# First convolution of a two-layer MoE network: the shared convolution in the turned image's PSUM banks, token logits from the finished image, top two of four by a 4x4 table

## What is computed

```python
# first convolution, on x normalised over channels per pixel
pooled = mean(x, (2, 3));  h = silu(pooled @ router_w1.T + router_b1)
probs = softmax(h @ router_w2.T + router_b2)            # 4 experts
top_v, top_i = top_k(probs, 2);  w = top_v / sum(top_v);  w = where(w >= 0.01, w, 0)
shared = silu(group_norm(einsum('oc,bchw->bohw', shared_w, x)))
expert_e = silu(group_norm(conv3x3(x, expert_w[e])))    # two of four are computed
x = x0 + shared + w0 * expert_{i0} + w1 * expert_{i1}
# first feed-forward network, on tokens (pixels) normalised over channels
probs = softmax(layernorm(t) @ router_w.T)              # 8 experts, two per token
gates = top2 / (sum(top2) + 1e-9)
y = sum over the two: gate * (silu(t w1) * (t w3)) w2
```

## Time and profile before

| | us |
|---|---|
| median of 3 runs | 2041.85 |
| lowest and highest | 2039.49, 2042.02 |
| the profiled execution | 2049.27 |
| its span on the core | 2047.5 |
| PE, DVE, ACT, POOL busy | 1725.7, 1474.9, 1029.6, 1055.8 |

### The profile page before, as it was taken

The page is one execution under the profiler, slowest core; times in us unless marked ns, Lnnn a source line. Parts: engine busy times, 40 slices in busy tenths (PEclk is TensorE's granted clock), DMA queues, the critical chain, the costliest instruction groups (busy, mean ns, idle before and its releaser), DMA issues.

```text
span 2047.5 us, 40915 instructions
## 1 busy us (share of the span) xinstructions
PE 1725.7 (84%) x9314; PEld 962.7 (47%) x9315; DVE 1474.9 (72%) x5423; ACT 1029.6 (50%) x1740; POOL 1055.8 (52%) x1198
## 2 busy tenths in 40 slices
PE   2679889988988849999999995589898959999957
PEld 2334444444444424555555552355555534444447
DVE  5777677776767656777777774777777657888857
ACT  1444344434434426777777773245656525555524
POOL 1003445435544646777777776435666444666620
PEclk8689999998999969999999998689989979999979
DMA  8600111111111124222222221312221013222146
GB/s 265 174 11 31 45 36 42 40 42 40 44 34 35 38 64 114 80 82 75 82 81 77 82 67 49 103 34 82 72 63 44 26 48 111 78 80 79 35 116 213
DMA packets 180063, 149.06 MB, mean 73 GB/s; under 512 B 19302, under 2 KB 161822, under 8 KB 179960
## 3 DMA queue, kind: packets, MB, share of 16 engines
q1 hardware_dynamic: 153336, 98.05, 17.5%
q0 software_dynamic: 26624, 49.93, 7.2%
HBM read 76.00 MB, written 77.34 MB: 75 GB/s over the span
## 4 chain that ended last, share of the span: by engine, by line
PE 54%; DVE 16%; issue 11%; ACT 9%; DMA 4%; POOL 3%; ACTq 1%; SPq 1%; DVEq 0%; POOLq 0%
PE banks L759 12%; PE banks L760 12%; PE banks L761 12%; PE banks L754 9%; PE banks L975 5%; ACT work L1091 4%; POOL slot_rows L626 2%; ACT work L1190 2%; PE banks L772 1%; DMA slot_rows<-work,small 1%; PE banks L985 1%; DVE small L1471 1%; DMA wb_h<-ffn_rows 1%; DVE small L1496 1%; DVE small L1467 1%
## 5 line engine op out<-in xcount | busy, mean ns | idle before, releaser
L647 POOL DMA_INDIRECT ffn_rows<-work x448 | 486.1, 1085 | 238.8 <-issue 170.0
L626 POOL DMA_INDIRECT slot_rows<-work,small x384 | 389.6, 1015 | 327.3 <-DVE small L1668 146.8
L754 PE MATMUL banks<-small,work 128*128 128x128 f32 x1344 | 197.3, 285 | 179.3 <-ACT work L1091 153.2
L754 PEld LDWEIGHTS banks<-small,work 128*128 128x128 f32 x1344 | 159.7, 146 | 251.4 <-issue 142.3
L1891 DVE TENSOR_TENSOR work<-work 128x512 f16<-128x512 f32 x376 | 260.8, 694 | 12.6
L759 PE MATMUL banks<-work,wb_h 128*128 128x512 f16 x648 | 247.4, 382 | 6.1 <-issue 4.5
L761 PE MATMUL banks<-work,wb_l 128*128 128x512 f16 x648 | 247.3, 382 | 0.0
L760 PE MATMUL banks<-work,wb_h 128*128 128x512 f16 x648 | 247.2, 382 | 0.0
L759 PE MATMUL banks<-work,wa_h 128*128 128x512 f16 x576 | 235.1, 408 | 3.6 <-ACT work L1122 3.2
L1907 DVE SCALAR_TENSOR_TENSOR work<-banks,small,work 128x512 f32<-128x512 f32 x216 | 161.4, 747 | 102.9 <-ACT work L1204 102.3
L760 PE MATMUL banks<-work,wa_h 128*128 128x512 f16 x576 | 234.5, 407 | 0.0
(11 more groups left out here) (323 smaller groups left out, 3203.2 us busy)
## 6 DMA issues: line engine op xcount, KB each, us to landing
wa_l<-slot_rows SPq DMA_DIRECT2D x112, 264.0 KB, 2.9
work<-ffn_rows SPq DMA_DIRECT2D x32, 512.0 KB, 5.3
work<-in_x SPq DMA_DIRECT2D x16, 512.0 KB, 3.4
ffn_rows<-small SPq DMA_DIRECT2D x32, 256.0 KB, 3.8
out_image<-work SPq DMA_DIRECT2D x16, 512.0 KB, 3.1
ffn_rows<-work POOLq DMA_INDIRECT x448, 2.2
slot_rows<-work,small POOLq DMA_INDIRECT x384, 2.3
slot_rows<-small SPq DMA_DIRECT2D x17, 264.0 KB, 4.2
```

The costliest lines, as they stand in the source:

```text
L626: pool_e.indirect_dma_start(slots, bass.IndirectOffsetOnAxis(ap=slot_i[:, row_buffer(p, i, k), tt:tt + 1], axis=0), rows[row_buffer(p, i, ...
L647: pool_e.indirect_dma_start(dst, bass.IndirectOffsetOnAxis(ap=idg[old.v][:, qq, 0:1].bitcast(I32), axis=0), yt[old.u][:, qq, :], None, bou ...
L754: last = pe.transpose(dst[:, tt * P:(tt + 1) * P], x, ident)
```

## The change

- The shared convolution (j = 0) now lands in `tp` (banks 0 and 1), by a new function `home(j)`; its statistics and SiLU read there. The next image's transposes now wait for that SiLU (`A_silu0`); the first expert convolution of the step waits for `A_silu1` of the image before in place of `A_silu0`.
- On PE a step now begins with the loads of the two expert numbers and two taps, then the transposes of the loaded image. The shared convolution of `nxt` stands ahead of the small product of its gates. `group_mean(old, 2)` stands behind four taps instead of three.
- Token logits: the router's weights are centred over channels once in the setup (three VectorE instructions, one transpose, one copy). The logits then come straight from the finished image `acc` right behind its transposes, and are multiplied by the token's 1/deviation on VectorE. `route_turn` and the ScalarE copy behind it (lines 1107) go, for stage A.
- Token choice: both picks are done in one chain on the logits themselves; the exponentials of all eight and of the second pick are one instruction behind it. The rest of the routing moved: the second pick from step i+1 to step i, the placing behind the image's statistics, woven with the last accumulation.
- Image gates: rank by a 4x4 table of differences; expert numbers, affine constants and exponentials picked in one product and one sum.
- On ScalarE the normalised tokens and their exponentials stand behind both SiLU instructions of the step instead of between.

```diff
+        def home(j):
+            return tp if j == 0 else pair[of(j)]
...
             def conv_half(i, j, half, regs, taps=range(TAPS)):
-                dst = pair[of(j)][:, half * 512:(half + 1) * 512]
+                dst = home(j)[:, half * 512:(half + 1) * 512]
...
+            def a_logits(i):
+                if some(i.b):
+                    pe.wait_ge(sem("A_pos_read"), i.b)
+                for tt in range(TPI):
+                    last = pe.matmul(sm_b[:, tt * E:(tt + 1) * E], acc[i.u][:, tt * P:(tt + 1) * P], rw_centred, start=True, stop=True)
+                last.then_inc(sem("A_logits_done"), 1)
...
             def a_step(i):
...
-                    turn(tp, [xcm[nxt.u][:, tt * P:(tt + 1) * P] for tt in range(TPI)]).then_inc(sem("A_xt_done"), 1)
                 if live(i, IMAGES):
                     pe.wait_ge(sem("A_gate_ready"), i.b + 1)
                     regs += [pe.value_load(eidx[0:1, i.u, k:k + 1], min_val=0, max_val=EC - 1) for k in range(2)]
-                    pe.wait_ge(sem("A_silu0"), i.b + 1)
-                    conv_half(i, 1, 0, regs, range(3))
+                    if some(i.b):
+                        pe.wait_ge(sem("A_silu1"), i.b)
+                    conv_half(i, 1, 0, regs, range(2))
+                if live(nxt, IMAGES):
+                    if some(nxt.b):
+                        pe.wait_ge(sem("A_silu0"), nxt.b)
+                    turn(tp, [xcm[nxt.u][:, tt * P:(tt + 1) * P] for tt in range(TPI)]).then_inc(sem("A_xt_done"), 1)
+                if live(i, IMAGES):
+                    conv_half(i, 1, 0, regs, range(2, 4))
                 if live(old, IMAGES):
                     group_mean(old, 2)
...
                     turn(tp, [acc[old.u][:, tt * P:(tt + 1) * P] for tt in range(TPI)]).then_inc(sem("A_tok_done"), 1)
+                    a_logits(old)
...
-                    conv_half(i, 2, 0, regs, range(5, 8))
+                    conv_half(i, 2, 0, regs, range(5, 7))
                 if live(nxt, IMAGES):
+                    pe.wait_ge(sem("A_padl_done"), nxt.b + 1)
+                    conv_half(nxt, 0, 0, regs)
+                    conv_half(nxt, 0, 1, regs).then_inc(sem("A_conv_done0"), 1)
                     pe.wait_ge(sem("A_hb"), nxt.b + 1)
...
-                if live(old, IMAGES):
-                    route_turn("A_", old)
-                if live(nxt, IMAGES):
-                    if some(nxt.b):
-                        pe.wait_ge(sem("A_silu1"), nxt.b)
-                    conv_half(nxt, 0, 0, regs)
-                    conv_half(nxt, 0, 1, regs).then_inc(sem("A_conv_done0"), 1)
...
-                if live(old, IMAGES):
-                    logits("A_", old, vec("rw0", 0, E))
...
             # ScalarE, a_step
-                if live(old, IMAGES):
-                    route_rows("A_", old)
...
                     a_silu(i, 1)
...
-                    route_copy("A_", old)
-                    route_exp("A_", old)
                     a_silu(nxt, 0)
                 if live(old, IMAGES):
+                    route_rows("A_", old)
+                    route_exp("A_", old)
...
             # VectorE, a_step
                 weave(has_old and group_affine(old, 2),
                       has_nxt and token_stats(lambda tt: tp_tok[:, tt, :], 1e-6, image_stats, sem("A_image_stats")),
-                      isinstance(i.b, int) and i.b == 0 and late_maxima(),
-                      has_older and route_rest(older))
-                weave(has_old and accumulate(old, 2, 0))
+                      isinstance(i.b, int) and i.b == 0 and late_maxima())
+                weave(has_old and accumulate(old, 2, 5),
+                      has_older and route_place(older))
...
-                weave(has and group_affine(i, 1))
+                weave(has and group_affine(i, 1),
+                      has_nxt and group_stats(nxt, 0))
                 weave(has_nxt and a_gates(nxt),
+                      has_nxt and shared_affine(nxt, 2),
                       has and accumulate(i, 1, 2),
-                      has_nxt and shared_job(nxt, 3),
-                      has_old and route_choose("A_", old, 2, 11))
+                      has_old and route_choose(old, 9))
```

## The result

The changed kernel takes 2052.09 us (median of 8 runs, 2048.06 to 2060.53) against 2041.93 us (8 runs): a ratio of 1.0054, 95% interval 1.0038 to 1.0070. The forecast was 2019 and faster. The profiled execution of the changed kernel took 2050.97 us, with a span of 2049.2.

A forecast was written before the change was run, and what follows sets the result against it. Stage A was taken as bound by a ring from engine to engine, with no engine full. 2041.85 less 11 us over six passes, 11 at stage A's end and half a microsecond for step 14 gave about 2019; range 2001 to 2040.

The forecast's parts named there:

- Low half to statistics, 15.05: First part of the inner step, VectorE's low half to the statistics of j = 2: 15.05 us against 15.2 before.
- hidden, just: ScalarE's two more table loads, 2 x 1.28 us, would be done about 1 us ahead of the SiLU of j = 2.
- the ring: Closed chain of waits from engine to engine in stage A, setting the step: 37.9 us inside a pass, 40.65 behind the jump.
- The jump's hold, 3.3 and half of the second: VectorE's idle time behind the loop's jump: 3.0 to 3.3 us, plus half of a second hold of 0.7 to 1.6.
- Setup 0 to 1 us: Setup gains four small instructions and loses a wait: 0 to 1 us, taken as 0.
- group mean's copy to the transposes: Third part of the step, from group mean's copy to the finished image's transposes: 9.0 us against 10.63, the gain of 1.6.
- The last stretch: Fourth part, finished image's transposes to next low half: 9.8 us (5.5 plus 4.2 of DVE), 11.4 with the clock loss.
- The bare register loads: On PE at the step's head, register loads no longer covered by transposes: 0.9 us, costing nothing while DVE is behind.
- The end of stage A: Image 15's scatters 26.8 us behind image 14's instead of 31.3; together 11 us gained, between 5 and 13.
- the clock takes it back: Rival: PE falls to 1.2 GHz behind the transposes in both steps of a pass, only the end pays; 2031, chance 0.17.
- VectorE's last weave is latency-bound: Slower rival: 27 woven instructions at 0.26 instead of 0.128 us add 3.5 us per step; 2068, chance 0.10 with the drain.
- The hold did not go: Rival that 52 fewer instructions remove the stop behind the jump: 3.6 + 0.8 us less per pass; 1993, chance 0.02.

The follow-up runs named there:

- f1_logits_late: On the changed kernel with both repairs (GpSimd's addition later, SiLU table early), the token logits moved on PE behind the normalised image's transposes; 2015.2 us, 0.9865.
- e4_both: The repaired kernel: the changed kernel with GpSimd's addition behind the token mask and SiLU's table loaded ahead of the jump; 2037.72 us, 0.9976.
- e1 to e4: Four edits of the changed kernel: GpSimd's addition cut to 8 columns (0.9967), addition later (1.0013), SiLU table early (1.0037), the last two together (0.9976).
- h1_before_lock: The kernel before the change, with one more GpSimd addition of 1024 columns behind the scatters for images 3 to 15; 2066.18 us, 1.0123.

## Why the prediction was wrong

**The forecast failed in four places, while the gain it bet on came inside a pass as it was priced.** The first of them put at nothing what GpSimd does beside VectorE. With most of GpSimd's addition left out (e1_add_tiny) the changed kernel is 18 us shorter, the most of any single edit on it. By its own steps:

- *Low half to statistics, 15.05.* This step failed. Measured 16.30 inside a pass; without the held comparison 14.54, so the count of instructions was itself half a microsecond too high, and that hid part of the miss. The working counted VectorE's instructions and their waits for semaphores, and never asked what GpSimd does meanwhile. The paragraph on GpSimd followed the scatters and passed over the addition behind them, which waits for the shared SiLU. The change moved that SiLU forward and the second pick, with two operands in SBUF, under it. In before's trace the addition stood at 450.50 and the statistics at 450.59: an addition of 2.35 us hidden under a reader of PSUM. The Trainium skill (SBUF — State Buffer, Who interferes with whom) states that a VectorE instruction with two SBUF inputs and a GpSimd instruction that reads SBUF exclude each other, and that the later one waits until the earlier is done. The trace agrees: 2.00 us held, end against end within 0.08 us, and a reduction with one input passed.
- *ScalarE, "hidden, just".* Right inside a pass (3.06 us to spare) and wrong behind the jump, where the load stands behind the wait: 1.28 us on the ring in those steps, so 10.27 where 9.0 was forecast. Before, no table had to be loaded there. The drain that the Trainium skill (ScalarE: Activation LUTs, What ACT_TABLE_LOAD costs) counts for a switch was not seen: 389.57 and 1.28 are 390.85, and the exponential starts at 390.87.
- *The jump's hold, 3.3 and half of the second.* Measured 3.75 to 4.16, 4.0 in the mean, and no second one in that place: 0.4 too little. Low half to statistics is 4.67 longer than inside a pass, which is 0.7 more than the hold. The hold comes on top of the held comparison and does not hide it. In the kernel before, the addition of GpSimd ran during the hold in these steps.
- *"Setup 0 to 1 us", and the written-out steps taken as before.* Wrong by 15.3 us, the largest single loss against the kernel before. (Against the forecast the step behind the jump is more: 44.66 for 40.65, five times, is 20 us.) The four intervals took 44.2, 46.2, 39.1 and 42.2 us for 39.5, 41.4, 38.2 and 37.5. I priced the steady step and never the first steps, where PE has little else to do, waits for everything, and so pays twice: for the order (the second image's transposes stand 13.1 us behind the first low half for 7.6, since the shared convolution's SiLU must have read `tp`) and for the clock. In the fourth interval the stretch from the finished image's transposes ran at a clock of 0.65 and took 14.48 us; before, 8.50 at 1.00:

```profile
231.45:245.93 14.48, 14.48 (x61) 9.26 (x62) 5.76 (x36) 2.39 (x4) 10.30 (x11) 0.65 0.14 48
```
```profile
223.71:232.21 8.50, 8.50 (x49) 4.88 (x50) 5.49 (x32) 2.39 (x4) 6.52 (x7) 1.00 0.16 53
```

  With the logits moved (f1_logits_late) the four intervals take 161.5 us for 168.5 in e4_both, so half of that loss is the logits' place and the clock. The first interval stays at about 44 to 45 us in every kernel that has the shared convolution in `tp`.

What held: group mean's copy to the transposes inside a pass, 9.0 for 8.92. The last stretch, 11.4 inside and 10.6 behind the jump, for 9.74 and 10.82: the sum over both steps is near (20.56 for 22.0), but the loss to the clock fell into the other step. The bare register loads (PE idle 1.10 us ahead of the first tap, for 0.9). The end of stage A: scatters of image 15 at 777.47, 26.1 us behind those of image 14 at 751.37, for 26.8; the whole end gained 8.2 us, within 5 to 13 but below 11.

Two sums of the prediction are slightly off and change nothing: 5.5 and 4.2 in its fourth part are 9.7 and not 9.8, and six passes have only five jumps back.

Of the rivals, *the clock takes it back* describes e1 to e4 well: a third to somewhat over half of what was expected of each repair did not come, and the last stretch grew. *VectorE's last weave is latency-bound* named the right place and the wrong mechanism: 27 woven instructions still came every 0.11 us (382.08 to 385.02), and the 2 us were one instruction. The hold did not go, as said.

A further error of reasoning is the place of the logits. I added 1.8 us of PE to the stretch in which VectorE waits for PE, and weighed it against a stretch of before that had lost 1.65 us to the clock (463.97) as if that loss were its rule; before's mean was 8.96 over these ten steps, not 9.63. Moving the logits by some products gives 14 us on the changed kernel and 23 on the repaired one.

## What to carry to other kernels

- Beside each VectorE chain that moves, lay out what GpSimd reads from SBUF at that time. Put its long instructions under VectorE instructions that read PSUM or a single operand; a tiny instruction can cost as much as the addition that it meets.
- A gain ahead of PE can be lost behind it: if PE arrives earlier only to wait 2 us, the following stretch can run slower. Look at the granted clock behind each wait, fill waits with products that nobody needs if the stretch behind is on the ring, and keep from that stretch all of PE's work that can stand elsewhere.
- Price the written-out first steps and the step behind a loop's jump apart from the steady one; a table load can be hidden in one and bare in the other. Where the program is short enough, write the loop out.

## What the runs showed of the hardware that I had not expected

- A VectorE instruction with two operands in SBUF is held until GpSimd's addition, which reads SBUF, is done: 0.22 us became 2.0 to 2.4 in the changed kernel and, with an unchanged VectorE program, in h1_before_lock.
- Behind a wait of 2.06 us on PE, 9.75 us of work took 13.24 us; 1.04 us of idle products in that wait, and as many in the one at group mean, undid it in this step, and in three of five such steps.
- The hold of VectorE behind a jump back, 2.7 to 4.3 us, did not follow the length of the body (524, 576 or twice as many instructions); where the jump was taken out there was none. With 524 instructions it was 3.5 to 4.3 us with GpSimd's addition where the change has it (or cut to 8 columns), and 2.7 to 2.9 with the addition later.
- A table load that is hidden in one step can be bare in the next, when a jump lies between the load's old place and its use. This depends on where the compiler puts it, and one SiLU of a single column ahead of the jump moved it.
